# The router logits' context share, from six TensorE products a tile to multiply-and-sum on VectorE

## The reference

```python
nx = _layer_norm(x, ln_gamma, ln_beta)
q = nx @ Wq
k = prototype_bank @ Wk
v = prototype_bank @ Wv
scores = jnp.einsum('bth,bph->btp', q, k) * H ** (-0.5)
weights = jax.nn.softmax(scores, axis=-1)
evidence = jnp.einsum('btp,bph->bth', weights, v)
anchor = jnp.broadcast_to(global_anchor[:, None, :], nx.shape)
combined = jnp.concatenate([nx, evidence, anchor], axis=-1)
router_logits = combined @ router_W + router_b
router_probs = jax.nn.softmax(router_logits, axis=-1)
...
routed = jnp.sum(expert_out * router_probs[..., None], axis=-2)
```

## Time and profile before

| what | value |
|---|---|
| median of 3 runs | 438.75 us (437.46 to 439.23) |
| span of the profiled execution | 436.9 us |
| TensorE busy | 422.1 us |
| VectorE busy | 296.3 us |
| ScalarE busy | 223.6 us |
| POOL busy | 175.0 us |

### The profile page before, as it was taken

How to read it: one execution, slowest core, us unless ns; L and a number is a source line. 1 busy time by engine, 2 the same in 40 slices (tenths; PEclk the granted TensorE clock), 3 DMA queues, 4 the chain that set the end, 5 groups by cost and what they waited for, 6 DMA issues and landing times.

```text
span 436.9 us, 9623 instructions
## 1 busy us (share of the span) xinstructions
PE 422.1 (97%) x3629; PEld 384.7 (88%) x3629; DVE 296.3 (68%) x748; ACT 223.6 (51%) x487; POOL 175.0 (40%) x184
## 2 busy tenths in 40 slices
PE   7899999999999999999999999999999899979996
PEld 6578999989998899889998899889988898868876
DVE  2785566674675696739863797389658755891797
ACT  2868643255347543764367246724672356326271
POOL 4545474553353526324523344344433632330020
PEclk9999999999999999999999999999999999998999
DMA  8786102531100210023000300030003021300301
GB/s 288 252 298 269 50 2 47 142 91 31 44 5 1 63 59 30 24 78 116 2 5 13 109 1 5 14 86 0 5 20 80 0 56 28 80 3 26 72 3 48
DMA packets 16837, 27.80 MB, mean 64 GB/s; under 512 B 3800, under 2 KB 9112, under 8 KB 16664
## 3 DMA queue, kind: packets, MB, share of 16 engines
q1 hardware_dynamic: 16664, 27.19, 21.2%
q10 hardware_dynamic: 128, 0.01, 0.0%
HBM read 15.94 MB, written 2.10 MB: 41 GB/s over the span
## 4 chain that ended last, share of the span: by engine, by line
PE 77%; DVE 15%; issue 3%; ACT 3%; DMA 1%; SPq 1%; ACTq 0%
PE hidden_banks L1688 7%; PE hidden_banks L1690 7%; PE hidden_banks L1689 7%; PE score_banks L1695 6%; PE score_banks L2060 5%; PE token_bank L1688 5%; PE token_bank L1689 5%; PE token_bank L1690 5%; PE score_banks L2030 4%; PE value_bank L2083 3%; PE value_bank L2086 3%; PE value_bank L1695 3%; DVE head_maxima L1463 3%; PE hidden_banks L1913 2%; DVE sums L1477 2%
## 5 line engine op out<-in xcount | busy, mean ns | idle before, releaser
L1620 POOL TENSOR_TENSOR hidden_low<-hidden,hidden_high 128x512 fp32r<-128x512 f32 x56 | 72.8, 1300 | 123.5 <-ACT hidden_high L1072 123.4
L1463 DVE TENSOR_REDUCE head_maxima<-score_banks 128x2 f32<-128x308 f32 x128 | 54.6, 473 | 17.1 <-PE score_banks L2030 15.0
L1688 PE MATMUL hidden_banks<-normed_high,hidden_w_high 128*128 128x256 f32 x224 | 64.2, 287 | 0.8 <-issue 0.8
L1689 PE MATMUL hidden_banks<-normed_high,hidden_w_low 128*128 128x256 f32 x224 | 62.5, 279 | 0.0
L1690 PE MATMUL hidden_banks<-normed_low,hidden_w_high 128*128 128x256 f32 x224 | 62.5, 279 | 0.0
L1132 ACT ACTIVATE exp_ring<-score_banks 128x512 f32<-128x512 f32 x96 | 52.6, 600 | 18.8 <-PE score_banks L2060 17.5
L1072 ACT CAST hidden_high<-hidden 128x512 fp32r<-128x512 f32 x56 | 34.8, 622 | 48.2 <-DVE hidden L1380 48.1
L1688 PE MATMUL token_bank<-expert_out_high,hidden_high 128*128 128x256 f32 x192 | 55.7, 290 | 0.0
L1064 ACT ACTIVATE hidden<-hidden_banks 128x512 f32<-128x512 f32 x56 | 33.3, 595 | 41.6 <-PE hidden_banks L1913 40.0
L1690 PE MATMUL token_bank<-expert_out_low,hidden_high 128*128 128x256 f32 x192 | 53.4, 278 | 0.0
L1689 PE MATMUL token_bank<-expert_out_high,hidden_low 128*128 128x256 f32 x192 | 53.4, 278 | 0.0
(11 more groups left out here) (294 smaller groups left out, 1111.5 us busy)
## 6 DMA issues: line engine op xcount, KB each, us to landing
unit_weights<-units SPq DMA_DIRECT2D x7, 768.0 KB, 6.0
query_stack<-queries_high SPq DMA_DIRECT2D x56, 64.0 KB, 2.0
tokens<-x SPq DMA_DIRECT2D x8, 256.0 KB, 3.7
query_stack<-queries_low SPq DMA_DIRECT2D x28, 64.0 KB, 2.0
w_slice<-units SPq DMA_DIRECT2D x7, 256.0 KB, 3.0
out<-tokens SPq DMA_DIRECT2D x7, 256.0 KB, 2.4
w_T<-folds SPq DMA_DIRECT2D x6, 256.0 KB, 6.1
pair_keys<-keys_high SPq DMA_DIRECT2D x16, 77.0 KB
```

What stands on the lines that cost most here:

```text
L1463: v.tensor_reduce(MX[:, s, first:first + step + 1:step], S[:, ring_of[key][0], 0:2 * CTX].rearrange("p (j n) -> p j n", j=2), AX.X, ALU.ma ...
L1620: nc.gpsimd.tensor_tensor(SL[:, ring(t, u), :], TB[:, ring(t, u), :], raw(SH[:, ring(t, u), :]), ALU.subtract).then_inc(gpsimd_h, 1)
L1688: mm(out_, lh, rh, start=start, stop=False, skip_group_check=skip)
L1689: mm(out_, ll, rh, start=False, stop=False, skip_group_check=skip)
```

## The change

The probabilities are also held token by token (`probs`, 128 tokens x 154). The change leaves the six products out and has VectorE multiply each token's row of probabilities with a row of 154 numbers for each expert (`router_rows`, the same in all 128 partitions) and sum the products into the logit, three experts times two halves: six instructions, each with a read of its sum. The rows are made on TensorE by six products of 128x154: for the first batch in `fold`, for the second in a new step `rows` at the start of tile 4's turn, whose result VectorE copies at the head of tile 4's logit step. In `fold` eight small products fall away for each batch, with the copies and splits behind them. The products of the multiplication (`router_terms`) lie over `x_hat0`, so POOL's `norm` waits for the logit step of the tile before. The slot of `logit` becomes 12.8 instead of 14.4. Some buffers move in SBUF.

```diff
@@ PLAN
-    "ln": 0.2, "norm": 1.6, "low": 6.6, "att": 7.9, "prob": 9.1, "route": 12.3, "logit": 14.4, "res": 17.4,
+    "ln": 0.2, "norm": 1.6, "low": 6.6, "att": 7.9, "prob": 9.1, "route": 12.3, "rows": 13.4, "logit": 12.8, "res": 17.4,
...
@@ buffers
+        TERMS = put("router_terms", [P, NSUB, EXPERTS, CTX], offset=xhat_at)
...
+        VR = put("router_rows", [P, EXPERTS, CTX])
...
@@ VectorE, fold
-                v.tensor_copy(VRF[:, 0, 0:EXPERTS], S[:, 0, 0:EXPERTS])
...
+                if b == 0:
+                    last = v.tensor_copy(VR[:, :, :], S[:, 0, 0:EXPERTS * CTX].rearrange("p (e n) -> p e n", e=EXPERTS))
+                last.then_inc(vector_fold, 1)
...
@@ VectorE, logit
-                dve.wait_ge(tensor_logit, upto(tensor_logit, key, "l"))
+                dve.wait_ge(gpsimd_prob, upto(gpsimd_prob, ("prob", t), "p"))
                 dve.wait_ge(vector_att, upto(vector_att, ("att", t), "t"))
-                parts_of = H[:, 0:8 * NSUB].rearrange("p (s i e) -> p i s e", i=2, e=4)
-                v.tensor_tensor(LG[:, :, :], LG[:, :, :], parts_of[:, 1, :, 0:EXPERTS], ALU.add).then_inc(vector_results, results.one())
-                dve.wait_ge(vector_results, results.n)
-                v.tensor_tensor(LG[:, :, :], LG[:, :, :], parts_of[:, 0, :, 0:EXPERTS], ALU.add).then_inc(vector_logit, 1)
+                dve.wait_ge(gpsimd_low, upto(gpsimd_low, ("low", t), "n"))
+                if t == 0:
+                    dve.wait_ge(vector_fold, upto(vector_fold, ("fold", 0), "VR"))
+                elif t == TPB:
+                    dve.wait_ge(tensor_rows, upto(tensor_rows, ("rows", 0), "r"))
+                    v.tensor_copy(VR[:, :, :], H[:, 0:EXPERTS * CTX].rearrange("p (e n) -> p e n", e=EXPERTS)).then_inc(
+                        vector_results, results.one())
+                    dve.wait_ge(vector_results, results.n)
+                for s in range(NSUB):
+                    for e in range(EXPERTS):
+                        last = v.tensor_tensor_reduce(out=TERMS[:, s, e, :], in0=PB[:, s, 0:CTX], in1=VR[:, e, :], scale=1.0,
+                                                      scalar=LG[:, s, e:e + 1], op0=ALU.mult, op1=ALU.add,
+                                                      accum_out=LG[:, s, e:e + 1])
+                last.then_inc(vector_logit, 1)
                 dve.wait_ge(vector_logit, upto(vector_logit, key, "l"))
...
@@ POOL, norm
                     pool.wait_ge(gpsimd_prob, upto(gpsimd_prob, ("prob", t - 1), "p"))
+                    pool.wait_ge(vector_logit, upto(vector_logit, ("logit", t - 1), "l"))
...
@@ TensorE
+            def router_rows(bank, b):
+                for e in range(EXPERTS):
+                    last = plain(bank[:, CTX * e:CTX * e + CTX],
+                                 [(RW[:, KC + k, e:e + 1].to_broadcast([P, P]), VL[b][:, k, 0:CTX]) for k in range(KC)])
+                return last
...
-            def logit(key):
...
```

More of the change, by code:

```diff
@@ L153 @@
         "prob": ["p"],
-        "logit": ["l"],
+        "rows": ["r"],
         "z": ["z"],
@@ L296 @@
     1: {
-        "logit": 15.4, "z": 0.62,
+        "z": 0.62,
     },
@@ L412, in schedule @@
             place(at + plan(t, "reload"), ("reload", t))
+    place(FIRST + LOOP * AGAIN + PLAN["rows"], ("rows", 0))
     return table
@@ L548, in build @@
         WS = put("w_slice", [P, 2, KC, UCOLS])
-        VTT1 = put("values_T1", [P, KC, P])
-        LT = [put(f"tail_rows{b}", [P, KC, 32]) for b in range(BATCH)]
-        SCW2, KTT, VTT0, OB, used0 = run(keys_at, [
+        VL1 = put("values_T1", [P, KC, P + 32])
+        SCW2, KTT, VL0, OB, used0 = run(keys_at, [
             ("query_score_w_raw", [P, KC, D], F32), ("keys_T", [P, KC, 160], F32),
-            ("values_T0", [P, KC, P], F32),
+            ("values_T0", [P, KC, P + 32], F32),
             ("out_b_row", [P, D], F32)])
@@ L563, in build @@
         SCW = [part[:, KC * 160:].rearrange("p (k n) -> p k n", k=KC) for part in (FW0, FW1)] + [SCW2]
-        VTT = (VTT0, VTT1)
+        VL = (VL0, VL1)
+        VTT = [part[:, :, 0:P] for part in VL]
+        LT = [part[:, :, P:P + 32] for part in VL]
+        at[0] += 256
         hidden_at = at[0]
@@ L637, in build @@
         WQR = put("query_w_raw", [P, KC, D])
-        XH1, NMH, NML, _ = run(setup_at, [("x_hat1", [P, NSUB, D], F32), ("max_high", [HEADS, TILE], F32R),
+        SUM, NMH, NML, _ = run(setup_at, [("sums", [P, TILE], F32), ("max_high", [HEADS, TILE], F32R),
                                           ("max_low", [HEADS, TILE], F32R)])
@@ L1589, in zeros @@
                 pool.wait_ge(tensor_vw, upto(tensor_vw, ("vw", 1, NU - 1), "m"))
+                pool.wait_ge(tensor_rows, upto(tensor_rows, ("rows", 0), "r"))
                 p.memset(raw(LKL[0][:, :, :]), 0.0).then_inc(gpsimd_zero, 1)
                 pool.wait_ge(tensor_prob, upto(tensor_prob, ("prob", LAST), "p"))
+                pool.wait_ge(vector_logit, upto(vector_logit, ("logit", LAST), "l"))
                 pool.wait_ge(tensor_att, upto(tensor_att, ("att", LAST), "s"))
@@ L2131, in _ @@
             parts = {"warm": warm_up, "fill": fill, "cv": context_v, "ck": context_k, "fold": fold, "vw": context_w, "vt": context_tail, "w2": w2, "cb": bias_out, "mod": mod, "bq": query_bias,
-                     "keyx": keyx, "key": pair_keys, "bias2": expert_bias, "norm": norm, "att": att, "prob": prob, "logit": logit,
+                     "keyx": keyx, "key": pair_keys, "bias2": expert_bias, "norm": norm, "att": att, "prob": prob, "rows": rows_again,
                      "za": hidden_first, "z": hidden, "p": second, "qx": qx, "query": query, "most": most, "row": row,
```

62 lines of the change are left out of this document (26 added, 36 removed).

## The result

The changed kernel takes 464.15 us (median of 4 runs, 461.53 to 467.93), the kernel before 438.2 us beside it: a ratio of 1.059, 95% interval 1.055 to 1.063. The profiled execution took 463.22 us, its span 461.4 us, 24.5 us more than in the earlier trace rows.

What follows compares the result with a forecast made beforehand. It took TensorE's in-order queue, busy 97% of the span, as the bound. Stalls and setup summed to 23.0 us, 31.5 with the clock; 436.9 + 31.5 = 468.4, plus 1.85 from span to median, gave 470 us, range 455 to 482.

Steps and rivals of the forecast that it cites:

- five places: Tiles 2 to 6, logit block ahead of the last two maxima: `row` transposes 3.4 us late on average.
- The block ahead of the last maxima: VectorE's logit block, 4.0 us, delays TensorE's transposes at five places, 17.1 us; tile 4's PSUM copy adds 0.6 us.
- the pair: One VectorE multiply-and-sum plus the read of its sum: 0.42 us, 2.5 us for six a tile.
- Tiles 7, 1 and 0: Tile 7's projection 1.6 us late, tile 1's gate products 1.8 us late, tile 0's block 1.6 us net.
- The lower clock: TensorE's clock falls behind each of the five stalls, 1.7 us each, 8.5 us in all.
- rival D: New stalls replace TensorE's other waits; even with all 14.8 us of idle gone, 447 us without the clock; chance 0.05.
- the setup: TensorE's six new 128x154 products, 1.7 us, replace eight small ones; net 1.0 - 0.7 = +0.3 us.
- the second context: TensorE's setup for the second batch: 0.68 us of small products go without replacement, counted as 0.7 us saved.
- Rival A: Stalls come at TensorE, but what runs after them stays at 2.4 GHz: 462 us; chance 0.20.
- Rival B: VectorE's multiply-and-sum runs at half rate, 0.18 us more for each of 48 pairs, 8.6 us: 479 us; chance 0.11.
- Rival C: VectorE's block ends before TensorE needs the maxima, so the products are saved and nothing waits: 436 us; chance 0.04.

Runs made afterwards that it cites:

- e6: Changed kernel with `router_terms` halved over `normed`, so POOL's `x_hat` does not wait for the sums; block at the change's place: 466.35 us, ratio 1.062.
- e9_fill_four: Changed kernel with 24 idle TensorE products ahead of the `row` transposes' wait for tiles 0, 2, 3 and 4: 457.36 us, ratio 1.046.
- e4: Changed kernel without the six multiply-and-sum instructions a tile, the logit step's place kept: 440.97 us, ratio 1.006.
- e12: Changed kernel with `router_terms` over `normed`, logit step cut in two, tile 7's second half and POOL's three clearings later: 437.07 us, ratio 0.9945.
- e2: Changed kernel with the logit step back at the place of the kernel before, POOL's `x_hat` still waiting for the sums: 464.62 us, ratio 1.061.
- e1: Changed kernel with the logit step right behind the last two maxima for tiles 2 to 6, not ahead of them: 458.59 us, ratio 1.044.
- e10: e6 with one more two-input 128x512 POOL instruction ahead of `x_hat`, beside the multiply-and-sums of tiles 2 to 6: 470.49 us, ratio 1.072.
- e3: Kernel before with only the logit step moved to the change's place, no multiply-and-sum and no new products: 446.28 us, ratio 1.017.

## Why the prediction was right, and where its sizes were off

The direction, the mechanism and its five places were right; 470 us was 6 us too much. On the spans the forecast was 31.5 us, the measurement 24.5 us. By the steps of the sum:

- *The block ahead of the last maxima, 17.1 + 0.6 us.* Measured net of the products saved, with the six new products that run inside the third stall: 17.1 - 5 x 0.59 + 1.7 = 15.8 us. The mis-sized term here is the pair: 0.30 us, not 0.42, as the read of the sum costs nothing beside the next multiply; 0.7 us less a place, 3.6 us in five. Two long pairs of 1.39 us gave back 2 x 1.02 = 2.0 us. They were not in the forecast.
- *Tiles 7, 1 and 0, 1.6 + 1.8 + 1.6 us.* New waits of TensorE: 1.39 us at the projection, 0.85 instead of 0.32 us at tile 1's gate, 1.22 us at L1896 and 0.26 us behind it for tile 0. Together 3.4 us, less 3 x 0.59 for the products saved, 1.6 us instead of 5.0. At tile 0 the wait is for POOL's `x_hat`, which stood still for the sums; I had priced that wait for tile 1 alone. e6 takes that wait away and gains nothing, since TensorE then waits longer for `context_w_low` from VectorE: 1.8 us instead of 0.26, and at tile 1's gate 2.08 us instead of 0.85.
- *The lower clock, 5 x 1.7 = 8.5 us.* Each fall cost 1.6 to 1.7 us, as the earlier trace rows had it, but there were four: 6.6 us by the windows. e9_fill_four took 6.8 us off by filling four stalls, so the price is shown by an edit and not only read; that the two numbers agree so closely is partly luck, given the spread. The count of four holds for the profiled execution. In the two slower runs, with 12.0 and 13.5 us missing by the clock, the five falls of the forecast or more are likely, at places that no trace shows.
- *What was swallowed.* The wait of 0.93 us for a DMA in the earlier trace rows is gone, 0.9 us of the 14.8 us of rival D.
- The sum of these is 15.8 + 1.6 + 6.6 - 0.9 = 23.1 us. The last 1.4 us, of which I had 0.3 us in the setup, can be found in the first 18 us: TensorE's wait for `normed` ends at 17.68 us instead of 16.27. Of that, 0.61 us stand ahead of the fold's products (10.13 instead of 9.52 us), where e6, with the same fold, has 8.88 us, so this part is spread of the runs; 0.8 us are the fold's new products. The 0.7 us that I had as saved for the second context were not followed.

Rival A's 462 us is nearer to the result than my own value, and yet its mechanism is false: the clock did fall. What I had too large (1.9 us at the block, 3.4 us at tiles 7, 1 and 0, 1.9 us at the clock) and the 0.9 us swallowed add up to 8.1 us, about the price that I had for the clock: its nearness is luck. Only the experiments part the two: e9 has the clock without the falls, e4 the place without the pairs. Rival B, half rate, fell: six pairs start 0.30 us apart, where the plain step of 128x154 takes 0.31 us. The Trainium skill, *Vector Engine (DVE) Microarchitecture Reference*, "Points that are easy to get wrong", states the halving for its form of instruction; this trace does not show it for this one. Rival C, that VectorE hides the work, is false for the change as it stands. For e12, in which the work stands where VectorE was idle, its forecast of 2.7 us less comes close (2.4 us less than the kernel before beside it), but part of that is the clock.

## What to carry to other kernels

In a queue that runs in order, ask first what stands behind a moved step and who waits for that; the price of the step comes after it. e2 and e1 show how a stall goes on to the next consumer, once through a shared buffer and once through the step that came next, so each place has to be followed on every queue. A step that waits for another engine in its middle can be cut there and its first half put into a gap: so placed, the same work cost 0.2% (0.0 to 0.4%), and with three clearings on POOL moved as well the version came out 0.55% faster, part of it by the clock.

## What the runs showed of the hardware

*VectorE waits for POOL.* In 18 places of the traces a multiply-and-sum of two SBUF tensors ran long beside a two-input 128x512 instruction of POOL (`hidden_low`, or the one added in e10): up to 1.50 us instead of 0.37, and each time it ended 0.17 to 0.18 us behind POOL's instruction. e10 brings it about on demand. It had been visible in other steps: `mean_var` takes 0.83 us at 132.26 in the kernel before, where POOL runs `hidden_low`, and 0.17 us at ten of its 18 places. The Trainium skill, *SBUF — State Buffer*, "Who interferes with whom", says that a VectorE instruction with two SBUF inputs and a GpSimd instruction that reads SBUF exclude one another. The trace agrees for `hidden_low` and for the added instruction. For `x_hat`, which reads SBUF as well, it agrees in part. Beside it pairs took 0.37 to 0.58 us, far less than `x_hat` itself. But where VectorE's `outs_low` (two SBUF tensors) was already running, POOL was the one that waited, and `x_hat` took 3.39 us instead of 2.44 (kernel before, timelines of VectorE and POOL):

```profile
165.93 1.27 DVE L1506 SCALAR_TENSOR_TENSOR outs_low<-outs_high,constants,outs_twice 128x1024 fp32r<-128x1024 f32 x1
...
166.13 3.39 POOL L1631 TENSOR_SCALAR x_hat<-tokens,mean_var,rstd 128x256 f32<-128x256 f32 x2
```

Two inputs on POOL's side are not enough either: beside POOL's `rstd` (two inputs, 128x2, about 0.8 us) the pairs took 0.37 to 0.38 us. Which property of POOL's instruction decides stays open.

*Not every stall lowers the clock.* Five waits of 1.1 us (e3) did not, four of the five of 2.6 to 3.9 us in the changed kernel did; the one of 3.24 us there and one of 3.33 us in e9 did not. The wait for a DMA that lowered it in the earlier trace rows, 1.67 us there, is in all 14 traces, 1.60 to 2.01 us long: it lowered the clock in nine of them and not in five. In e3 it is as long, 1.67 us, and the clock holds (TensorE's timeline and windows):

```profile
400.58 0.98 PE L2060 MATMUL score_banks<-query_stack,pair_keys 100*128 100x256 f32 x6 [1.67 <-DMA query_stack<-max_low]
...
400.00:402.00 2.00, 1.42 (x11) 1.00 0.01 1
402.00:404.00 2.00, 2.00 (x19) 1.00 0.40 135
```

e3's only fall came in the setup, behind a wait of 0.98 us that is in the kernel before too and lowered nothing there. The length of the idle time alone does not decide it; what else does stays open here. The falls are also a good part of the spread of the runs: spans of 459.6 and 461.4 us came with a mean granted clock of 0.981, one of 465.4 us with 0.971.
